# Graph kernel: start stores, hops without a barrier, later gathered sums, and a new end

## The reference

```python
h = L0(x, edge_attr_64, [src, dst], ...)      # 4 heads: exp(clip(K[src]*Q[dst]*E)) * V[src], summed per dst
x = layernorm(x + h)
h = mean of x and three hops: x_k+1 = segment_sum(w * x_k[src], dst),  w = dis[src] * dis[dst]
x = layernorm(x + h)
h = L2(x, attn_w): softmax over each node's edges of leaky_relu(s_src + s_dst), weighted sum, elu
x = layernorm(x + h)
h = L3(x, edge_attr_2, ...): z = x @ W_fc.T; a = leaky_relu(u[src] + v[dst] + edge term + moments)
    # softmax per dst; sum of p * (z[src] + W_e2n @ (W_edge @ e)) / sum of p
x = layernorm(x + h)                          # the output, (3125, 64) fp32
```

## Time and profile before

| | us |
|---|---|
| median of 3 runs | 2179.7 |
| lowest, highest | 2173.67, 2180.04 |
| the profiled execution | 2178.74 |
| its span (first to last instruction) | 2176.9 |
| busy in it: PE | 1449.8 |
| busy: DVE | 1385.2 |
| busy: POOL | 1269.4 |
| busy: ACT | 994.1 |

### The profile page before, as it was taken

How to read it: one execution, slowest core, us unless ns; L and a number is a source line. 1 busy time by engine, 2 the same in 40 slices (tenths; PEclk the granted TensorE clock), 3 DMA queues, 4 the chain that set the end, 5 groups by cost and what they waited for, 6 DMA issues and landing times. The chain is left out here.

```text
span 2176.9 us, 44484 instructions
## 1 busy us (share of the span) xinstructions
PE 1449.8 (67%) x13123; PEld 1228.5 (56%) x13123; DVE 1385.2 (64%) x3503; ACT 994.1 (46%) x2236; POOL 1269.4 (58%) x1362
## 2 busy tenths in 40 slices
PE   3466776666676676676429918815649778968792
PEld 3355555555555555555329908813638667867682
DVE  4787777777777777777776678743364435444544
ACT  4354444454454454454229117701056555646560
POOL 0777777777777777777300013500777777777740
PEclk8788888888888888888759968955557777767675
DMA  6333333333333333333100000011232222222210
GB/s 112 77 85 84 80 79 83 80 78 84 79 79 83 80 78 84 80 78 82 29 1 2 0 2 2 2 38 17 59 84 48 48 48 57 48 48 48 38 17 16
DMA packets 125314, 120.60 MB, mean 55 GB/s; under 512 B 83887, under 2 KB 89558, under 8 KB 125066
## 3 DMA queue, kind: packets, MB, share of 16 engines
q0 software_dynamic: 39072, 66.01, 14.8%
q1 hardware_dynamic: 67028, 48.96, 7.8%
q10 hardware_dynamic: 19094, 4.08, 0.9%
HBM read 113.29 MB, written 5.65 MB: 55 GB/s over the span
## 5 line engine op out<-in xcount | busy, mean ns | idle before, releaser
L687 POOL DMA_INDIRECT shared<-kv_tab,idx x784 | 765.1, 976 | 290.2 <-issue 238.6
L880 PE MATMUL bank<-key_hot,lo_hot 128*128 128x350 f16 x784 | 189.1, 347 | 301.5 <-DVE count L749 229.7
L2086 POOL DMA_INDIRECT count<-att_tab,count x320 | 315.5, 986 | 97.5 <-issue 97.5
L880 PEld LDWEIGHTS bank<-key_hot,lo_hot 128*128 128x128 f16 x784 | 56.1, 98 | 391.5 <-issue 375.8
L749 DVE TENSOR_TENSOR count<-count,bank 128x350 f32 x392 | 205.3, 524 | 82.1 <-issue 45.8
L813 ACT ACTIVATE lo_dist<-iota_neg,tile_lo 128x128 f16<-128x128 f32 x784 | 238.5, 389 | 0.0
L2286 ACT ACTIVATE shared<-shared 128x128 f32<-128x128 bf16 x352 | 144.9, 482 | 137.0 <-PE bank L2363 132.4
L734 DVE TENSOR_SCALAR key_hot<-iota_key,tile_key 128x350 f16<-128x350 f16 x784 | 195.8, 321 | 0.0
L2397 PE MATMUL bank<-count,tab 128*66 128x88 f32 x1100 | 131.2, 303 | 52.3 <-DVE count L2203 52.3
L2397 PEld LDWEIGHTS bank<-count,tab 128*66 128x66 f32 x1100 | 128.6, 194 | 52.6 <-DVE count L2203 52.6
L755 DVE TENSOR_TENSOR prod<-bank,shared 128x512 f32<-128x512 f32 x98 | 67.8, 692 | 139.9 <-DMA shared<-kv_tab,idx 131.2
(11 more groups left out here) (441 smaller groups left out, 3162.8 us busy)
## 6 DMA issues: line engine op xcount, KB each, us to landing
shared<-in_edge_attr SPq DMA_DIRECT2D x97, 256.0 KB, 3.1
shared<-kv_tab,idx POOLq DMA_INDIRECT x784
shared<-lo_tab SPq DMA_DIRECT2D x22, 512.0 KB
count<-att_tab,count POOLq DMA_INDIRECT x320
qwin<-q_tab ACTq DMA_DIRECT2D x196, 16.0 KB
count<-v_win SPq DMA_DIRECT2D x1, 2352.0 KB, 9.1
g_edge<-att_tab,count POOLq DMA_INDIRECT x110
kv_tab<-count SPq DMA_DIRECT2D x1, 1600.0 KB, 7.2
```

What stands on the lines that cost most here:

```text
L687: nc.gpsimd.indirect_dma_start(kv[:, s, c, :], None, kv_tab, bass.IndirectOffsetOnAxis(ap=idx[:, s, c:c + 1], axis=0)).then_inc(kv_in[s], 16)
L880: last = nc.tensor.matmul(bank[6 + q % 2][:, 0:KC], lo_hot[:, c, :], key_hot[:, c, :], start=i == 0, stop=i == GT - 1)
L2086: nc.gpsimd.indirect_dma_start(ring[s][:, j, 0:D + 2], None, att_tab[1], bass.IndirectOffsetOnAxis(ap=src_i[:, t:t + 1], axis=0)).then_inc ...
```

## The change

Four edits.

1. In the first block the seven weight loads come first on SP, then `kv_tab` alone. ACT issues `q_tab` and its tail, then does the `lo_rows` copy and the zeros. The three `edge_tab` rows and `lo_tab` are issued by ACT at the head of the layer 0 sweep.
2. The hops are unrolled. `parts` and `parts_new` are used in turn, the copy is gone, DVE signals each finished pair and PE waits for a pair only where the first tile of a hop needs it. The last hop makes no new parts. One DVE copy per pair is gone, and `total` comes last.
3. In layer 3 each gathered unit moves one to two iterations later: units 0 to 2 go with iteration 0, unit 25 with 21, unit 26 with an added place behind the last iteration. Their arguments and one-hots stand at the end of the iteration on DVE, their sum behind `block_sum` on PE. The semaphores of this part are cleared and freed behind it.
4. The end is one block. DVE builds a matrix `back` (98 x 65) that turns rows back and adds the edge attributes' share at once; PE multiplies with it. DVE takes four groups of seven tiles from the banks: maximum, reciprocal, multiply, add to x. The layernorm's shift, last product and stores go in two parts (14 and 11 tiles), squares are on ACT. ACT stores the first part, SP the rest.

```diff
+                by_tile = "(t p) f -> p t f"
+                sp.wait_ge(s_taken, len(MM0))
+                sp.dma_start(kv_tab.rearrange(by_tile, p=P), tab[:, :, :]).then_inc(s_stored, 16)
...
-                nc.scalar.activation(lo_rows.rearrange("p (k e) -> p k e", k=TB), lo_f, ACT.Copy).then_inc(s_lo, 1)
+                act.wait_ge(s_taken, len(MM0))
+                act.dma_start(q_tab[0:NP, :].rearrange(by_tile, p=P), qt[:, :, :]).then_inc(s_stored, 16)
+                act.wait_ge(s_ones, 1)
+                act.dma_start(q_tab[NP:NP + W, :], tmp[0:W, 0, :]).then_inc(s_stored, 16)
+                nc.scalar.activation(lo_rows.rearrange("p (k e) -> p k e", k=TB), lo_f, ACT.Copy)
...
+                for i, t in enumerate((tile_lo[:, :, :].rearrange("p g c -> p (g c)"), tile_hi[:, :, :].rearrange("p g c -> p (g c)"), tile_dst)):
+                    act.dma_start(edge_tab[i], t).then_inc(kept, 16)
+                act.dma_start(lo_tab.rearrange("(k r) e -> r k e", r=P), lo_rows.rearrange("p (k e) -> p k e", k=TB)).then_inc(kept, 16)
...
-                    with pe.Fori(0, 3) as k:
-                        pe.wait_ge(x_ok, k + 1)
-                        pass_on(pe)
+                    pe.wait_ge(x_ok, 1)
+                    for k in range(3):
...
+                                    if k > 0 and m % len(HG) == 0 and i == 0 and h % 2 == 0:
+
+                                        pe.wait_ge(x_ok, 1 + (k - 1) * len(HG) + h // 2 + 1)
...
+                            if k < 2:
+                                into = both[(k + 1) % 2][:, w, :, :]
+                                nc.vector.tensor_tensor(qt[:, w, :], rows[:, w, 0:D], bc(dis[:, w], 2, D), ALU.mult)
+                                dve.drain()
+                                nc.vector.tensor_copy(into[:, :, 0, :], qt[:, w, :])
+                                dve.drain()
+                                nc.vector.tensor_tensor(into[:, :, 1, :], qt[:, w, :], into[:, :, 0, :], ALU.subtract).then_inc(x_ok, 1)
                             nc.vector.scalar_tensor_tensor(total[:, w, :], rows[:, w, 0:D], 1.0 / HOP_SCALE, total[:, w, :], ALU.mult, ALU.add)
...
-                        nc.vector.tensor_copy(parts[:, :, :, :], parts_new[:, :, :, :])
-                        dve.drain().then_inc(x_ok, 1)
...
-        beside_of = [[j for j in range(NPU) if j * ND // NPU == i] for i in range(ND)]
+
+        beside_of = [[j for j in range(NPU) if max(0, min(ND, -(-(17 * j - 48) // 18))) == i] for i in range(ND + 1)]
...
+                        for j in beside_of[i]:
+                            logits_p(j)
+                        for j in beside_of[i]:
+                            hots_p(j)
                     add_sums(ND - 1)
+                    for j in beside_of[ND]:
+                        logits_p(j)
+                    for j in beside_of[ND]:
+                        hots_p(j)
+                    add_sums(ND)
...
                         edge_sum(i)
+                        block_sum(i)
                         for j in beside_of[i]:
                             gathered_sum(j)
-                        block_sum(i)
...
+                nc.vector.scalar_tensor_tensor(back[:, 0:D], e2n_rep[:, 0, :], mask_of[0], ident[:, 0:D], ALU.mult, ALU.add)
+                dve.drain()
+                nc.vector.scalar_tensor_tensor(back[:, 0:D], e2n_rep[:, 1, :], mask_of[1], back[:, 0:D], ALU.mult, ALU.add).then_inc(back_ok, 1)
...
+                        last = nc.tensor.matmul(bank[k][:, j * (D + 1):(j + 1) * (D + 1)], acc[0:ME, t * P:(t + 1) * P], back[0:ME, :], start=True, stop=True)
...
+                    nc.vector.tensor_scalar(stat[:, 0, w], ps[:, :, D], 1e-30, None, ALU.max)
                     dve.drain()
+                    nc.vector.reciprocal(stat[:, 1, w], stat[:, 0, w])
+                    dve.drain()
+                    nc.vector.tensor_tensor(tmp[:, w, :], ps[:, :, 0:D], bc(stat[:, 1, w], 2, D), ALU.mult)
+                    dve.drain()
+                    nc.vector.tensor_tensor(xrow[:, w, :], xrow[:, w, :], tmp[:, w, :], ALU.add)
...
+                for k, w in enumerate(halves):
+                    act.wait_ge(shift_ok, k + 1)
+                    nc.scalar.activation(xrow[:, w, :], tmp[:, w, :], ACT.Square).then_inc(square_ok, 1)
+                act.wait_ge(var3, 1)
+                nc.scalar.activation(stat[:, 0, :], stat[:, 3, :], ACT.Sqrt).then_inc(std3, 1)
+                act.wait_ge(out_ok, 1)
+                act.dma_start(out[0:2 * RT * P, :].rearrange(by_tile, p=P), xrow[:, 0:2 * RT, :]).then_inc(stored, 16)
```

More of the change, by code:

```diff
@@ L1084, in build @@
         HG = [range(t, min(t + 2, NT)) for t in range(0, NT, 2)]
+        both = (parts, parts_new)
         x_ok, agg_ok, agg_used = sem("hop_rows"), sem("hop_sum"), sem("hop_sum_used")
@@ L2229, in _ @@
                     logits_d(0)
-                    for j in beside_of[0]:
-                        logits_p(j)
                     hots_d(0)
@@ L2429, in build @@
         attention("l3", att_tab[1], D + 4, True, general3, prepare=(edge_terms, moments_act, moments_pe))
-        summed = short_sem("e_summed")
-        five = [range(t, t + 5) for t in range(0, NT, 5)]
         ME = EA_AT + 2
+        back = work_diag[:, 0, 0, 0:D + 1]
+        mask_of = [work_diag[:, 0, 1, k:k + 1] for k in range(2)]
+        back_ok, summed, shift_ok, square_ok, var3, std3, out_ok, stored = (
+            short_sem(f"o_{n}") for n in ("matrix", "summed", "centred", "squared", "variance", "deviation", "rows", "stored"))
+        sevens = [range(t, min(t + RT, NT)) for t in range(0, NT, RT)]
+        halves = [slice(0, 2 * RT), slice(2 * RT, NT)]
         with nc.Block() as block:
@@ L2435, in _ @@
             def _(pe):
-                for k, ts in enumerate(five):
+                pe.wait_ge(back_ok, 1)
+                for k, ts in enumerate(sevens):
                     for j, t in enumerate(ts):
-                        last = nc.tensor.transpose(bank[k][:, j * ME:(j + 1) * ME], acc[0:ME, t * P:(t + 1) * P], ident[0:ME, 0:ME])
+                        last = nc.tensor.matmul(bank[k][:, j * (D + 1):(j + 1) * (D + 1)], acc[0:ME, t * P:(t + 1) * P], back[0:ME, :], start=True, stop=True)
                     last.then_inc(summed, 1)
@@ L2442, in _ @@
             def _(dve):
-                for k, ts in enumerate(five):
+                for k in range(2):
+                    nc.vector.tensor_tensor(mask_of[k], ident[:, D + 2 + k:D + 3 + k], ident[:, EA_AT + k:EA_AT + k + 1], ALU.add)
+                nc.vector.tensor_copy(back[:, D:D + 1], ident[:, D + 1:D + 2])
+                dve.drain()
+                nc.vector.scalar_tensor_tensor(back[:, 0:D], e2n_rep[:, 0, :], mask_of[0], ident[:, 0:D], ALU.mult, ALU.add)
+                dve.drain()
@@ L2447, in _ @@
                     dve.drain()
-                    into = rows[:, ts[0]:ts[-1] + 1, D + 2:D + 4]
-                    nc.vector.tensor_tensor(into, into, ps[:, :, EA_AT:ME], ALU.add)
-        def l3_before(dve, aux_in, aux_ok):
-            for k in range(2):
-                nc.vector.tensor_tensor(total[:, :, :], bc(rows[:, :, D + 2 + k], 2, D), bc(e2n_rep[:, k, :], 1, NT), ALU.mult)
+                    nc.vector.reciprocal(stat[:, 1, w], stat[:, 0, w])
+                    dve.drain()
+                    nc.vector.tensor_tensor(tmp[:, w, :], ps[:, :, 0:D], bc(stat[:, 1, w], 2, D), ALU.mult)
@@ L2456, in l3_before @@
+                    dve.drain()
+                    nc.vector.tensor_tensor(xrow[:, w, :], xrow[:, w, :], tmp[:, w, :], ALU.add)
                 dve.drain()
[L2457 removed]
+                nc.vector.tensor_reduce(stat[:, 0, :], xrow[:, :, :], AX.X, ALU.add)
                 dve.drain()
[L2459 to L2462 removed]
@@ L2463, in build @@
-        stored = sem("out_stored")
-        with nc.Block() as block:
+                nc.vector.tensor_scalar(stat[:, 1, :], stat[:, 0, :], 1.0 / D, None, ALU.mult)
+                dve.drain()
+                for w in halves:
+                    nc.vector.tensor_tensor(tmp[:, w, :], xrow[:, w, :], bc(stat[:, 1, w], 2, D), ALU.subtract).then_inc(shift_ok, 1)
+                for k, w in enumerate(halves):
+                    dve.wait_ge(square_ok, k + 1)
+                    nc.vector.tensor_reduce(stat[:, 2, w], xrow[:, w, :], AX.X, ALU.add)
@@ new lines, in _ @@
+                dve.drain()
+                nc.vector.tensor_scalar(stat[:, 3, :], stat[:, 2, :], 1.0 / D, EPS, ALU.mult, ALU.add)
+                dve.drain().then_inc(var3, 1)
+                dve.wait_ge(std3, 1)
+                nc.vector.reciprocal(stat[:, 1, :], stat[:, 0, :])
+                dve.drain()
+                for w in halves:
+                    nc.vector.tensor_tensor(xrow[:, w, :], tmp[:, w, :], bc(stat[:, 1, w], 2, D), ALU.mult).then_inc(out_ok, 1)
+            @block.scalar
@@ new lines, in _ @@
+            def _(act):
+                for k, w in enumerate(halves):
+                    act.wait_ge(shift_ok, k + 1)
```

(2 more changed lines are left out.)

73 lines of the change are left out of this document (31 added, 42 removed).

## The result

| | before | after |
|---|---|---|
| median of the runs | 2176.68 (2170.96 to 2180.04) | 2124.87 (2122.41 to 2130.23) |
| ratio, 95% interval | | 0.9768 (0.9737 to 0.9799) |
| the profiled execution, its span | 2178.74, 2176.9 | 2125.83, 2123.9 |
| busy: PE, DVE, POOL, ACT | 1449.8, 1385.2, 1269.4, 994.1 | 1427.7, 1357.8, 1270.2, 1000.0 |

What follows compares the result with a forecast made beforehand. Each place has its own pacer: POOL in the sweep and layer 3, PE's rests in the hops, a DVE chain at the end. 2.5 + 13.5 + 30 + 8.5 = 54.5 off 2178.74 gave 2124, range 2114 to 2137.

Steps and rivals of the forecast that it cites:

- hops: Between hops, PE's rest shrinks from 4.53 to 1.1 us and the clock stays up: 13.5 us gained.
- layer 3: Only the last gathered unit's own chain follows its landing, so the part ends at 2105.3 instead of 2135.4: 30 us gained.
- start: Layer 0 sweep begins 4.4 us earlier, part given back to stores beside its gathers: 2.5 us gained.
- end: Last block: product with `back`, layernorm in halves, earlier stores, less 0.8 for clearing semaphores: 8.5 us gained, bounds 4.5 and 11.5.
- The 2 that I gave back for gathers beside stores: Layer 0 sweep: 1.4 MB of stores beside the first gathers slow them by 2 us, which stay.
- Rival B: DMAs are not faster issued from two engines: no gain at start, none in output; 2128.5, chance 0.06.
- The spare: Layer 3: PE has 10 us to spare before the last gathered unit lands.
- rival A: PE becomes the bound in layer 3, iterations take 22.3 us at clock 0.67: 2136, chance 0.10.
- my upper price: End: the product with `back` takes 11.2 us if all 25 tiles run slow, against 8.1 taken.
- the other value, 1.2: End: by the skill's page, 1.2 us of a table load between squares and Sqrt would show; by the row it hides.
- Rival C: Layer 3: the last sum still waits for more than its own unit, no gain there: 2154, chance 0.02.
- rival D: Slower than before: PE without its five rests stays at 1.2 GHz through layer 3's loop: 2257, chance 0.03.

Runs made afterwards that it cites:

- start_filled: Changed kernel with q_tab's tail issued behind the zeros, some stores moved to the block that ORs the counts, five idle PE transposes: 2120.85, ratio 0.9737.
- old_units: Changed kernel with the old list of gathered units per iteration, the new places in the order kept: 2127.81, ratio 0.9776.
- dense23: Changed kernel with 23 dense and 26 gathered units instead of 22 and 27: 2107.33, ratio 0.9677.
- only_end: Kernel before with the new one-block end alone, including the clearing of semaphores: 2169.86, ratio 0.9979.
- only_late: Kernel before with only layer 3's gathered units one to two iterations later, their sum behind the block's: 2149.08, ratio 0.9878.
- only_hops: Kernel before with only the hops unrolled, no copy, and per-pair signals: 2166.48, ratio 0.9957.
- turn_warm: Changed kernel with the `back` product moved into the layer 3 block and 60 idle PE matmuls in the wait for the last unit; slower chip, no time given.
- only_start: Kernel before with only the new order of stores and weight loads in the first block: 2176.5, ratio 1.002.

## Why the forecast was right

The forecast was 2124 and the median 2124.87. The two large terms, hops and layer 3, hold, and so the size of the gain does. That it came within 1 us is luck: start and end together fell 7.5 short (2.5 forecast and -1.2 measured, 8.5 and 4.7), and 2.0 more in the hops and 3.7 that no term foresaw made up for 5.7 of it.

*Start* (2.5 forecast, nothing or a loss measured). The failing steps are the tail's issue, 6.67 where I took 4.4 from two issues of 3.91 and 4.92, and the first index load's landing, 4.2 behind its issue against 2.5 before, which I had not priced. Four stores were issued beside it, but with one beside it in start_filled it was still 3.9, so their number is not what does it. The 2 that I gave back for gathers beside stores was wrong the other way, it is 0.1. Rival B's mechanism held at this place: with `q_tab` issued from ACT beside `kv_tab`, `kv_tab` landed 10.4 behind its issue instead of 7.2 and `q_tab` 11.2 instead of 10.6, so both were down by 46.2 (45.8 before). This is what the Trainium skill says (DMA: Bandwidth & Descriptors, section "Issuing engines are not separate DMA queues"): transfers started by different engines share the same 16 DMA engines, and only the time of issuing is saved. start_filled shows the way out, which is to put the held issue beside other work.

*Hops* (13.5 forecast, 15.5 in the profile, 13 against the loop's shorter form). The rest came out at 0.79 for my 1.1, the clock stayed up (1.00), as I took it. What I missed is that the first hop can differ by 1.5 by itself: I called it fixed at 37.86, and it is 36.3 to 36.7 in nine of ten traces with unrolled hops and 37.3 in the tenth, and 36.3 to 36.4 in two with the loop. I also read the loop's first pass as "no slower than the others", where the earlier trace rows have 37.86 and 37.18. That unrolling adds no wait is true all the same.

*Layer 3* (30 forecast, 30.1 measured). From the landing to the end 5.1 forecast, 5.05 measured. The spare was forecast as 10 and is 12.3. But this was right for a part of the reason only: I had the iteration at 20.4 and took the list of units to be needed. The new place alone does it (old_units), and with it an iteration takes 18.1 (dense23), at a higher clock. So rival A was further off than I held it. The clock was 0.84 in one such stretch (0.93 in the 60 us from 1820 on) and 0.72 in a lower one, against 0.74 in the first of the earlier trace rows:

```profile
1800.00:1820.00 20.00, 17.74 (x201) 15.75 (x200) 10.83 (x35) 13.96 (x37) 15.12 (x17) 0.84 0.25 56
1940.00:1960.00 20.00, 18.39 (x181) 17.30 (x180) 11.16 (x35) 13.60 (x35) 15.31 (x16) 0.72 0.25 55
...
2100.00:2104.00 4.00, 4.00 (x21) 4.00 (x20) 2.47 (x7) 0.00 (x0) 0.00 (x0) 0.50 0.00 0
```

*End* (8.5 forecast, 6.2 in the block and -1.5 in the passage, 4.7; the forecast's lower bound was 4.5). The product took 10.93, my upper price, because all of it ran at 0.50 (the last line above is a stretch of it) and not just 9 tiles; x was whole after 13.5 where I took 11.5. (My sum of 9 slow and 16 fast tiles is 7.9, not 8.1.) Behind the addition the block gained 2.3 of the 3.4 forecast, 1.2 in the layernorm and 1.1 in the stores. The clearing, priced at 0.8, costs nothing (only_end), while the passage behind the late last unit is 1.5 to 1.95 longer, which I had not seen. What makes it longer is open: it is there without the clearing (only_late), and with the last unit inside an ordinary iteration it is 6.95 (dense23) or 7.90 (old_units). The table load before Sqrt hid, as the row let expect, and nothing of the other value, 1.2, showed: 1.28 at 2114.00, Sqrt at 2115.54, right when DVE's sums were done.

*What made up for it.* 3.7 between the hops and the last landing. It is the store of `v_tab`, 4.1 sooner than in the trace of before; other kernels with the same edits don't have that, so I call it chance. Rival C fell with the 5.05, rival D with iterations that kept POOL's pace at these clocks.

## What to carry to other kernels

Where one engine paces a loop, ask what stands behind its last delivery and put everything else ahead. Here the place within the iteration did it, and putting work off by another iteration or two added nothing that could be measured. When the order has taken a wait out, price the iteration anew: the room it left (two more dense units, with another start and the product inside some 45 us) was worth nearly as much as the change. A long issue of a DMA cost nothing beside a long instruction of the same engine, so put it there.

## What the runs showed of the hardware that I had not expected

- The first block's products ran at a clock of 1.00 in twelve profiles and fell to 0.50 in two (only_hops, turn_warm), 6.8 us for nothing in the first of them, and the times of only_start and only_hops fall into two groups 6 to 8 us apart. Differences of a few us need the profile's stages, not the median alone.
- A clock at 1.00 for 15 us of work fell to 0.50 one us into a product of 98 x 65 tiles, with PE at work throughout; a rest of 2.22 between hops of 128 x 128 matmuls left it at 1.00. Rests alone don't tell what the clock does.
- The issue of a store right behind the one of a 3200-row table was held: 3.91 us for `q_tab` itself behind `kv_tab`, and for the small tail behind `q_tab` 4.92 on SP, 5.58 and 6.67 on ACT. Behind the output's 24 tiles the last tile's took 2.80, behind 10 tiles 1.25.
- The mean clock over the same layer 3 work was 0.73 in one order of instructions (before) and 0.84 in another (only_late).
- One chip ran the kernel before in 3016 us instead of 2175. Traces of other kernels there show the same durations of instructions as elsewhere and longer waits between engines.
